# The first transfers and the first norm of a two-layer gated cross-attention network in another order

## The reference, cut to what matters

```
x = x + tanh(g_xattn[0]) * cross_attention_0(layernorm(x), ctx)     # 16 heads of 16
x = x + tanh(g_ffn[0])   * mixture_of_8_experts(layernorm(x))       # top 1
x = x + tanh(g_xattn[1]) * cross_attention_1(layernorm(x), ctx)     # with rms norms of q and k
x = x + tanh(g_ffn[1])   * self_attention_and_mixture_of_16(layernorm(x))
```

## Time and profile before

| | |
|---|---|
| median of 3 runs | 819.42 us (817.55 to 819.58) |
| profiled execution | 822.67 us, of which the span of the profile is 820.9 us |
| TensorE busy | 761.7 us, 93% of the span |
| VectorE, ScalarE, GpSimd busy | 430.3, 352.7, 231.1 us |
| mean granted TensorE clock | 0.963 |
| DMA | 58.29 MB, mean 71 GB/s |

### The profile page before, as it was taken

One profiled execution on the slowest core, in us unless ns is written; L12 is line 12 of the kernel. 1 busy time (PEld: TensorE's weight loads), 2 busy tenths in 40 slices (PEclk: granted clock), 3 DMA queues, 4 the chain that ended last, 5 costly groups with the idle time before them and its releaser, 6 DMA issues.

```text
span 820.9 us, 13560 instructions
## 1 busy us (share of the span) xinstructions
PE 761.7 (93%) x4626; PEld 621.6 (76%) x4627; DVE 430.3 (52%) x831; ACT 352.7 (43%) x852; POOL 231.1 (28%) x284
## 2 busy tenths in 40 slices
PE   7998899999849985999999999999898999999996
PEld 5887755666537863898898898898686888888885
DVE  6688262111446876345445435436545566656564
ACT  3887302222137874445445455455542233333332
POOL 5110040000355425221321321310423334343430
PEclk9999789999968998999999999999989999999999
DMA  8960031111100002101100110000113334343421
GB/s 318 420 232 2 1 103 46 45 46 37 53 19 2 2 2 76 41 20 34 45 26 32 34 36 32 25 14 1 58 39 91 98 109 118 105 122 101 130 74 51
DMA packets 25670, 58.29 MB, mean 71 GB/s; under 512 B 3600, under 2 KB 14480, under 8 KB 24352
## 3 DMA queue, kind: packets, MB, share of 16 engines
q1 hardware_dynamic: 24864, 55.68, 21.0%
q0 software_dynamic: 768, 2.10, 0.8%
HBM read 51.67 MB, written 6.09 MB: 70 GB/s over the span
## 4 chain that ended last, share of the span: by engine, by line
PE 81%; ACT 6%; DVE 4%; DMA 3%; POOL 2%; issue 2%; POOLq 0%; SPq 0%; PEldq 0%; ACTq 0%; PEld 0%; DVEq 0%
PE PS L329 15%; PE PS L331 15%; PE PS L330 15%; PE PS L1374 7%; PE PS L1099 6%; PE PS L1114 3%; PE PS L441 3%; PE PS L432 2%; PE PS L399 2%; PE PS L405 2%; PE PS L1380 2%; ACT x_probT L523 1%; PE PS L387 1%; ACT x_prob L552 1%; PE PS L454 1%
## 5 line engine op out<-in xcount | busy, mean ns | idle before, releaser
L329 PE MATMUL PS<-tTh,wh 128*128 128x512 f32 x200 | 79.9, 399 | 0.0
L889 ACT ACTIVATE hhh<-hh 128x512 fp32r<-128x512 f32 x50 | 31.6, 632 | 112.2 <-DVE hh L915 100.6
L330 PE MATMUL PS<-tTl,wh 128*128 128x512 f32 x200 | 79.3, 397 | 0.0
L331 PE MATMUL PS<-tTh,wl 128*128 128x512 f32 x200 | 79.3, 397 | 0.0
L513 DVE TENSOR_TENSOR hhl<-hh,hhh 128x512 fp32r<-128x512 f32 x50 | 52.6, 1052 | 34.9 <-ACT hhh L889 34.9
L1481 ACT ACTIVATE sm<-sm,nmx 128x128 f32<-128x128 f32 x128 | 49.7, 391 | 37.5 <-DVE nmx L1538 37.5
L971 POOL TENSOR_TENSOR wl<-wraw,wh 128x512 fp32r<-128x512 f32 (+1 forms) x50 | 58.2, 1163 | 8.4 <-POOL wh L969 7.9
L513 DVE TENSOR_TENSOR oTl<-PS,oTh 128x512 fp32r<-128x512 f32 x32 | 22.1, 692 | 71.6 <-ACT oTh L1475 71.6
L969 POOL CAST wh<-wraw 128x512 fp32r<-128x512 f32 (+1 forms) x50 | 26.1, 521 | 118.2 <-PE PS L331 113.3
L1577 POOL CAST ah<-araw 128x512 fp32r<-128x512 f32 (+1 forms) x32 | 16.6, 518 | 145.0 <-PE PS L331 143.1
L1099 PE MATMUL PS<-WE,xsT 128*128 x120 | 56.4, 594 | 0.1
(11 more groups left out here) (241 smaller groups left out, 1848.4 us busy)
## 6 DMA issues: line engine op xcount, KB each, us to landing
WE<-moe SPq DMA_DIRECT2D x8, 1536.0 KB, 13.8
wraw<-moe SPq DMA_DIRECT2D x25, 384.0 KB, 3.1
araw<-attn SPq DMA_DIRECT2D x16, 384.0 KB, 3.1
cwb<-cw_d SPq DMA_DIRECT2D x20, 256.0 KB, 3.8
WX<-wx SPq DMA_DIRECT2D x2, 1024.0 KB, 8.5
avraw<-attn_v SPq DMA_DIRECT2D x8, 256.0 KB, 3.1
xs_d<-zeros SPq DMA_DIRECT2D x1, 1920.0 KB, 15.9
xs_s<-xs_d SPq DMA_DIRECT2D x15, 128.0 KB, 2.1
```

Of the source, the lines that this page charges most:

```text
L329: nc.tensor.matmul(out, wh_, xh_, start=first, stop=False, **kw)
L330: nc.tensor.matmul(out, wh_, xl_, start=False, stop=False, **kw)
L331: return nc.tensor.matmul(out, wl_, xh_, start=False, stop=last, **kw)
L889: nc.scalar.activation(hhh[half][:, :], hh[half][:, :], ACT.Copy).then_inc(s.hi_done, 1)
```

## The change

SP issues x of batch 0 alone (128 KB) and ctx of batch 0, then gates, x of batches 1 to 3 (384 KB), vecs, ctx of batch 1, the output matrix Wo (256 KB), x of batches 4 to 7 (512 KB), ctx of batches 2 and 3, and the rest as before. ScalarE issues the other matrices at its start: Wk, then cols, Wq, Wv, 256 KB each but cols. TensorE waits for each matrix where it first uses it, and fills 10 times instead of 24. The first norm has three groups instead of two (batch 0; 1 to 3; 4 to 7). xn of batches 0 and 1 is made by VectorE, not by GpSimd. VectorE clears the PSUM banks ahead of the constants of the routing, and sets those constants only behind the statistics of batches 4 to 7, which wait for the last part of x, and ahead of xattn_dve.

```diff
@@ xattn_pe
             def keys(b):
                 pe.wait_ge(s.ctx_in[b % CTX], 16 * (b // CTX + 1))
+                if b == 0:
+                    pe.wait_ge(part_in[0], 16)
...
             if L == 0:
                 pe.wait_ge(Es.zeroed, 1)
-                fill(24, 0)
+                fill(10, 0)
                 pe.wait_ge(psum_zeroed, 1)
-                pe.wait_ge(wx_in[0], 16)
...
@@ xattn_pool
-            power(pool, "ln1" if L == 0 else "ln3", 0)
-            normed(0)
-            normed(1)
-            power(pool, "ln1" if L == 0 else "ln3", (EARLY, FIRST)[L])
+            if L == 0:
+                power(pool, "ln1")
+                power(pool, "ln1", 1)
+                power(pool, "ln1", EARLY)
+                pool.wait_ge(s.ln_done, 2)
+            else:
...
@@ xattn_sp
-            load(0)
-            sp.dma_start(WX[0][:, :, :], wx_d[0]).then_inc(wx_in[0], 16)
-            sp.dma_start(cols[:, :, :].rearrange("p a c -> p (a c)"), col_d).then_inc(col_in, 16)
+            sp.dma_start(gates[:, :], gate_d.partition_broadcast(P)).then_inc(gate_in, 16)
+            load_x(sp, 1)
             sp.dma_start(vecs[:, 0:2, :].rearrange("p a d -> p (a d)"), vec_d[0:2 * D].partition_broadcast(P)).then_inc(vec_in, 16)
-            for b in range(1, CTX):
+            load(1)
+            sp.dma_start(WX[0][:, :, 3 * D:4 * D], wx_d[0][:, :, 3 * D:4 * D]).then_inc(part_in[3], 16)
+            load_x(sp, 2)
+            for b in range(2, CTX):
                 load(b)
...
+        X_PARTS = ((0, 1), (1, EARLY), (EARLY, B))
...
@@ block.scalar
+            for k in (0, 2, 1):
+                act.dma_start(WX[0][:, :, k * D:(k + 1) * D], wx_d[0][:, :, k * D:(k + 1) * D]).then_inc(part_in[k], 16)
+                if k == 0:
+                    act.dma_start(cols[:, :, :].rearrange("p a c -> p (a c)"), col_d).then_inc(col_in, 16)
             act.wait_ge(gate_in, 16)
@@ block.vector
             ch.link(v.memset(mhalf[:, :], -0.5))
+            v.memset(PS[:, 4:8, :], 0.0).then_inc(psum_zeroed, 1)
+            v.memset(xb0.v17[:, :, :, XD:XD + 1], 1.0)
+            dve.wait_ge(const_done, 3)
+            ch.link(v.tensor_reduce(pair_rows[:, :], head_rows[:, :].rearrange("p (a k) -> p k a", k=2), AX.X, ALU.add))
+            dve.sem_inc(pairs_done, 1)
+            dve.wait_ge(x_in[0], 16)
+            ch.link(v.bn_stats(st[:, 0, :], X[:, 0, :]))
+            moments(ch, 0, 1)
+            dve.wait_ge(col_in, 16)
+            v.tensor_tensor(masked_bk[:, :, :], cols[:, 0, :].unsqueeze(2).broadcast_to([P, C, 2]), pair_rows[:, :].unsqueeze(1).broadcast_to([P, C, 2]), ALU.mult).then_inc(bias_done, 1)
+            powered(dve, "ln1")
+            ln_scale(xb0.xn[0][:, :], X[:, 0, :], 0).then_inc(xs[0].ln_done, 1)
+            dve.wait_ge(x_in[1], 16)
+            for b in range(1, EARLY):
+                i = v.bn_stats(st[:, b, :], X[:, b, :])
+            ch.link(i)
+            moments(ch, 1, EARLY)
+            dve.wait_ge(vec_in, 16)
+            dve.wait_ge(tg_done, 1)
+            v.tensor_scalar(vec("bo0"), vec("bo0"), tg[:, 0:1], None, ALU.mult).then_inc(xs[0].bo_scaled, 1)
+            powered(dve, "ln1", 1)
+            ln_scale(xb0.xn[1][:, :], X[:, 1, :], 1).then_inc(xs[0].ln_done, 1)
+            dve.wait_ge(x_in[2], 16)
+            for b in range(EARLY, B):
+                i = v.bn_stats(st[:, b, :], X[:, b, :])
+            ch.link(i)
+            moments(ch, EARLY, B)
             ch.link(v.memset(upto[:, :, :], 0.0))
             for e in range(E0):
                 v.memset(expert_ids[:, e:e + 1], float(e))
                 v.memset(upto[:, e, 0:e + 1], 1.0)
             for j in range(SLOTS):
                 v.memset(tile_ids[:, j:j + 1], float(j))
-            ch.link(v.memset(xb0.v17[:, :, :, XD:XD + 1], 1.0))
-            v.memset(PS[:, 4:8, :], 0.0).then_inc(psum_zeroed, 1)
             for e in range(E0):
                 ch.link(v.memset(rank8[:, e:e + 1], float(E0 - e)))
```

More of the change, by code:

```diff
@@ L232, in build @@
         cw_d = nc.dram_tensor("cw_d", (E1, T), F32).ap()
-        x_in = [sem("x_in0"), sem("x_in1")]
+        x_in = [sem(f"x_in{i}") for i in range(3)]
+        part_in = [sem(f"part_in{i}") for i in range(4)]
         gate_in, vec_in, late_in, out_done = sem("gate_in"), sem("vec_in"), sem("late_in"), sem("out_done")
@@ L413, in queries @@
                 read("xT", b)
+                if L == 0 and b == 0:
+                    pe.wait_ge(part_in[2], 16)
                 columns("Q", b, 2 * D, m_.xT)
@@ L469, in output @@
                 read("cxT", b)
+                if L == 0 and b == 0:
+                    pe.wait_ge(part_in[3], 16)
                 rows("O", b, 3 * D, m_.cxT)
@@ L496, in xattn_pe @@
                         queries(n + 2)
+                        if n + 2 == 0:
+                            pe.wait_ge(part_in[1], 16)
                         rows("V", n + 2, D, m_.cT[(n + 2) % CTX])
@@ L589, in build @@
         EARLY, MOST, FIRST = B // 2, B - 2, 2
-        POWERS = [("ln1", 0, EARLY), ("ln1", EARLY, B), ("ln2", 0, MOST), ("ln2", MOST, B), ("ln3", 0, FIRST), ("ln3", FIRST, B),
+        POWERS = [("ln1", 0, 1), ("ln1", 1, EARLY), ("ln1", EARLY, B), ("ln2", 0, MOST), ("ln2", MOST, B), ("ln3", 0, FIRST), ("ln3", FIRST, B),
                   ("ln4", 0, MOST), ("rms1", 0, MOST), ("ln4", MOST, B), ("rms1", MOST, B), ("rms2", 0, EARLY), ("rms2", EARLY, B)]
@@ L682, in normed @@
                     pool.wait_ge(s.turn_done, turn_no[L]["xT", b - 2] + 1)
-                powered(pool, "ln1" if L == 0 else "ln3", 0 if b < (EARLY, FIRST)[L] else (EARLY, FIRST)[L])
+                if L == 0:
+                    powered(pool, "ln1", 1 if b < EARLY else EARLY)
+                else:
+                    powered(pool, "ln3", 0 if b < FIRST else FIRST)
                 ln_scale(m_.xn[b % 2][:, :], X[:, b, :], b, nc.gpsimd).then_inc(s.ln_done, 1)
@@ L702, in queries @@
                 nc.gpsimd.tensor_tensor(q_scale[:, b:b + 1], q_mean[:, b:b + 1], mhalf[:, 0:1], ALU.pow).then_inc(s.q_power, 1)
-            power(pool, "ln1" if L == 0 else "ln3", 0)
-            normed(0)
-            normed(1)
-            power(pool, "ln1" if L == 0 else "ln3", (EARLY, FIRST)[L])
+            if L == 0:
+                power(pool, "ln1")
+                power(pool, "ln1", 1)
+                power(pool, "ln1", EARLY)
+                pool.wait_ge(s.ln_done, 2)
+            else:
+                power(pool, "ln3", 0)
+                normed(0)
+                normed(1)
+                power(pool, "ln3", FIRST)
             if L:
@@ L1639, in attn_sp, with load_x @@
             load_heads(AH // 2 - 1)
+        X_PARTS = ((0, 1), (1, EARLY), (EARLY, B))
+        def load_x(sp, k):
+            b0, b1 = X_PARTS[k]
+            sp.dma_start(X[:, b0:b1, :], x_d[b0:b1].rearrange("b s d -> s b d")).then_inc(x_in[k], 16)
         @block.sync
         def _(sp):
[L1644 to L1647, removed]
+            load_x(sp, 0)
+            sp.dma_start(xb0.cT[0][:, :, :], ctx_d[0]).then_inc(xs[0].ctx_in[0], 16)
             xattn_sp(sp)
```

## The result

The changed kernel takes 823.24 us (median of 8 runs, 820.33 to 826.17), the kernel before 819.42 (8 runs): ratio 1.0053, 95% interval 1.0029 to 1.0077. It is slower by about 4 us, where I had forecast no change (−0.2).

The account below looks back on a forecast made before the run. TensorE bounds from 21.07 us; before that, VectorE's in-order queue behind x_in[2] sets the first maximum. Landing 10.95 + 4.4 = 15.35 instead of 15.54, clock cancelling: 819.42 − 0.2 = 819.2 us; range with rivals 816.4 to 822.0.

Parts of the forecast that it names:

- the 4.4 summed from rows: VectorE's work between the last x landing and first maximum: statistics 2.02, memsets 1.9, values 0.42 and 0.06 us.
- the landing of x_in[2]: When the last 512 KB of x arrives for VectorE: taken as 10.95 us, between bounds of 10.1 and 12.35.
- the 2.25: Time gates and cols together cost, worked out from vecs' landing; 0.85 us of it was kept in the changed kernel.
- the 10.1 us without stalls: Lower bound for the last x landing: 2.63 MB at 375 GB/s to 9.3, seen 0.8 us later.
- the stall: Low transfer rate from 5.0 to 6.0 us, 131 then 39 GB/s, where gates takes its turn on SP's queue.
- the fourth rival: Nothing of the transfer stall is hidden, x_in[2] lands at 12.35: +1.2 us, 820.6; chance 0.12.
- The second term: TensorE's clock around batch 1's scores: half clock expected too, effects taken to cancel, from −1.7 to +1.2 us.
- Rival 2: TensorE's clock stays down after 5 us idle, still 0.5 at 28 us: +2 to +5.7, about 823; chance 0.12.
- 1: Half clock falls wholly into TensorE's idle time before batch 1, x_in[2] lands at 10.1: −2.7 us, 816.7; chance 0.09.
- 3: x_in[2] lands before 8, VectorE's maximum follows the scores at 11.5 to 12.7: −3 to −4, about 815.8; chance 0.05.
- the break-even (11.1): Landing of x_in[2] at which VectorE's first maximum starts as before: 15.54 − 4.4 = 11.1 us.

Follow-up runs that it names:

- whole-matrix kernel: The changed kernel with all four matrices in one 1,024 KB transfer behind cols on ScalarE's queue; ratio to the kernel before 1.0028.
- one-queue run: The changed kernel with the three matrices and cols issued on SP's queue between the parts of x, none on ScalarE's; ratio 1.0043.
- the six: Six kernels, the changed one among them, with the same transfers in the same order up to the last part of x; landing 12.3 to 13.6, ratios 0.9967 to 1.0064.
- three orders: The changed kernel with constants ahead of the last x wait, its statistics behind the first softmax, xn of batch 1 before bo0; ratio 0.9968.
- the kernel with the order mended: The changed kernel with cols and gates packed into Wk's transfer, vecs copied per partition, and VectorE's queue ordered as in three orders; ratio 0.9997.

## Why the prediction was wrong

**Right.** The kernel is bound as described: VectorE's in-order queue behind x_in[2] sets the first maximum, and the steady step keeps its 8.55 us. The interval from the start of the statistics to the maximum was 4.33 us (13.50 to 17.83) for the 4.4 summed from rows. The 5.5 us from maximum to second scores, the first transposes (6.35 for "near 7"), fills that cost nothing: all as written. The scores of batch 0 started at 12.35, later than the 10 to 11.5 given; Wq made TensorE wait until 10.21 (I had 7.5) and vecs came at 10.33, but both were hidden.

**The step that failed** is the landing of x_in[2]: 10.95 taken, with 12.35 as the worst case, and 13.48 and 12.81 measured. It is the term of the sum "I take 0.85 of the 2.25": over the 10.1 us without stalls it was 3.4 and 2.7 us. That put the maximum at 17.83 instead of 15.35. What was wrong in it, as far as the runs show:

- I read the stall from rows that ended at 6.0. In the trace of the kernel before it lasts another microsecond, with the DMA engines 0.44 busy:

```profile
6.00:7.00 1.00, 1.00 (x6) 0.80 (x5) 1.00 (x4) 0.00 (x0) 0.00 (x0) 1.00 0.44 135
```

- I let the second queue fill 1.4 us of the stall. It fills something at times (0.31 MB from 5 to 6 us in the whole-matrix kernel), but not here. From 3 to 5 us both queues had bytes to move, and the rate was half; as I read it cols held up the one while gates held up the other. Packing both away raised 184 GB/s to 380.
- The stall is not a fixed time: doubling gates cost the next transfer 3.5 us.
- I put the 2.25 us down to gates and cols alone, though I had worked it out from the landing of vecs, and counted vecs by its bytes. It is a slow transfer of its own, and the part of the loss that stands clearest: the landing is 12.4 with it and 10.9 and 11.4 without.
- The sum lets x_in[2] land when the bytes ahead of it are through. The changed kernel had moved as much as those 2.63 MB by 11.3 us (2.65 MB), but by the landing at 13.48 it had moved 3.46 MB: transfers that stand behind it in the queue moved before it was complete. Why is not shown.

With all three small or broadcast transfers gone the landing is 10.90 and 11.38. That it meets my 10.95 is luck: the 10.95 held 0.85 us for a stall, and without one the sum says 10.1. The rule that I set beside it (Trainium skill, DMA: Bandwidth & Descriptors, section Issuing engines are not separate DMA queues) speaks for the fourth rival. The one-queue run does not contradict it, 13.86 for 12.3 to 13.6, but one landing does not show it either; the rival's own 12.35 was too early for all but the earliest of the six.

**The second term** is the clock, which I let cancel. TensorE was at half clock through the whole of the second scores, +0.91 us, and the transposes (3.60 for 3.48), +0.12. I had TensorE stand some 5 us in one piece, from 15.8 on. It stood twice: 2.49 us until 17.97, since the value rows of batch 1, which I had let follow the scores at once, waited for x_v in VectorE's queue, and 3.61 us ahead of the second scores. The clock fell between 18 and 19 us, behind the first of the two, where in the kernel before it fell at 22, behind the 2.50 us that end at 21.07. Rival 2's mark, 0.5 at 28 us, was met to the letter (0.51), but only because everything ran later by then: the clock was back at 29, when the transposes ended, and the rest of that step ran at full speed. So against the kernel before: 2.29 (maximum) + 0.91 + 0.12 = 3.3, the 3.35 seen in the steady step.

This second part is not a fixed price of a late maximum. From the maximum to the third scores it is 14.62 us in the kernel before, 15.68 in the changed kernel and 16.03 in its repeat, but 14.64 with one queue, where the maximum is the later one (18.21) and TensorE idles 4.04 us before the second scores, and 13.34 in three orders. So the zero that I took for the clock lies within what these kernels show; what decides it, no run here shows.

**The rivals.** 1 and 3 did not happen. 4 had the mechanism and too small a price. Of 2 only the part up to the transposes happened, 1.0 us of its 2 to 5.7. My chance of 0.13 for slower was too small, since the break-even (11.1) stood less than 0.2 us from the value that I took, and every doubt about it (1 KB pieces, two queues, small transfers) pointed to later.

## What to carry to other kernels

A wait placed in an in-order queue delays all that stands behind it: before you bring the first transfer forward, look at which engine gets the *last* one's wait, and what it does next. Here 4.0 us of statistics and constants, none of which the first batch needed, stood between the last transfer and the first softmax; setting the constants ahead of the wait and taking the statistics behind the softmax turned +0.5% into −0.3%, with the transfers as they were. Price transfers in their place in the queue: the byte count gave 10.1 us; without the three small or broadcast transfers it was 10.9 and 11.4, with them 12.3 to 13.6.

## What the runs showed of the hardware that I had not expected

- In the whole-matrix kernel, with a transfer of 128 pieces of 16 bytes, all read from one place, at the head of the only queue that had work left, all 16 DMA engines all but stopped for a microsecond (0.04 busy, 1 GB/s from 6 to 7 us) with 1.3 MB behind it.
- With a transfer of 256 KB in which all partitions read the same 2 KB the rate was 140 GB/s for a microsecond at 93% busy (141 in the kernel with the order mended); with a copy for each partition it was 386 (383). Whether the one address is the cause, or something else of the access, no run separates.
- The spans of one kernel go with the mean granted clock: among the changed kernel's eight runs 0.966 and 0.967 go with 818.6 to 820.2 us, 0.964 with 820.9, 0.958 to 0.960 with 822.0 to 824.4. An early shift of 3 us is about what the profiled execution gained in the routing stage alone, at 0.70 instead of 0.50 in the same 16 us.
